# Block quantisation of the FFN weights: all vector passes on VectorE, the rounding constant in one ScalarE pass

## The reference

```python
def _quantize_elem(x, ebits, mfrac, max_norm):
    ax = jnp.abs(x)
    priv = jnp.floor(jnp.log2(jnp.where(ax == 0, 1.0, ax)))
    priv = jnp.maximum(priv, float(-2 ** (ebits - 1) + 2))
    scale = jnp.exp2(priv - mfrac)
    return jnp.clip(jnp.round(x / scale) * scale, -max_norm, max_norm)

def _quantize_mx(x, ebits, mfrac, emax_elem, max_norm):
    xb = x.reshape(shp[:-1] + (shp[-1] // 32, 32))
    amax = jnp.max(jnp.abs(xb), axis=-1, keepdims=True)
    sexp = jnp.floor(jnp.log2(jnp.where(amax == 0, 1.0, amax))) - emax_elem
    scale = jnp.exp2(jnp.clip(sexp, -127, 127))
    return (_quantize_elem(xb / scale, ebits, mfrac, max_norm) * scale).reshape(shp)

def _q_w(w): return _quantize_mx(w, 2, 1.0, 2.0, 6.0)
gate = einsum(_q_act(x), _q_w(w_gate)); up = einsum(_q_act(x), _q_w(w_up))
out = x + einsum(_q_act(silu(gate) * up), _q_w(w_down))      # w_gate, w_up: 2048 x 512, w_down: 512 x 2048
```

## Time and profile before

| | us |
|---|---|
| time, median of 3 runs | 645.82 |
| lowest and highest of the 3 | 642.88, 647.63 |
| span of the profiled execution (first to last instruction) | 645.2 |
| front, to the first weight unit on DVE | 30.0 |
| step 0 | 47.7 |
| steps 1 to 6 | 294.0, or 49.0 each |
| from step 7's start to the first matmul of the FFN | 47.3 |
| FFN | 226.3 |

### The profile page before, as it was taken

The page is one execution under the profiler, slowest core; times in us unless marked ns, Lnnn a source line. Parts: engine busy times, 40 slices in busy tenths (PEclk is TensorE's granted clock), DMA queues, the critical chain, the costliest instruction groups (busy, mean ns, idle before and its releaser), DMA issues.

```text
span 645.2 us, 11064 instructions
## 1 busy us (share of the span) xinstructions
PE 512.5 (79%) x2992; PEld 322.8 (50%) x2992; DVE 567.9 (88%) x951; ACT 387.4 (60%) x803; POOL 388.1 (60%) x391
## 2 busy tenths in 40 slices
PE   1799688777599789689599785569998899889984
PEld 1375565655575665565475653424444444344431
DVE  1347899999999999999999999669999999999994
ACT  2478778787678788688687777323334333343332
POOL 6367577687678678677677677643343434444443
PEclk9958768688778588688777687679999999999997
DMA  5220303203203203212312101010111000210020
GB/s 158 99 99 20 113 19 123 87 15 118 84 15 116 81 30 106 89 33 98 98 33 98 65 1 46 5 49 2 33 48 49 33 33 33 65 33 33 33 65 34
DMA packets 25479, 38.48 MB, mean 60 GB/s; under 512 B 4848, under 2 KB 8944, under 8 KB 25456
## 3 DMA queue, kind: packets, MB, share of 16 engines
...
...
## 4 chain that ended last, share of the span: by engine, by line
issue 31%; DVE 31%; PE 25%; ACT 9%; POOL 2%; DVEq 1%; DMA 1%; POOLq 0%; ACTq 0%; SPq 0%
PE psA L1168 5%; PE psA L1194 5%; PE psA L1359 3%; PE psC L1136 3%; DVE wam L884 3%; DVE f L932 2%; PE psC L1227 2%; DVE qam L884 2%; ACT Dt L684 2%; DVE CT L956 2%; DVE wn L912 2%; DVE qs L887 2%; DVE qinv L890 2%; PE psC L1218 1%; PE psC L1376 1%
## 5 line engine op out<-in xcount | busy, mean ns | idle before, releaser
L587 POOL TENSOR_TENSOR qd<-qc,qs 128x512 bf16<-128x512 bf16 x64 | 67.1, 1048 | 121.4 <-DVE qc L1104 121.4
L828 ACT ACTIVATE wraw<-psA 128x512 f32<-128x512 f32 x64 | 38.1, 598 | 107.4 <-PE psA L1359 105.5
L1194 PE MATMUL psA<-vp,CT 128*128 128x33 f32 x512 | 83.3, 320 | 24.3 <-DVE CT L956 24.1
L1194 PEld LDWEIGHTS psA<-vp,CT 128*128 128x128 f32 x512 | 80.4, 243 | 29.6 <-issue 17.6
L1168 PE MATMUL psA<-qbd,kT 128*128 128x512 f32 x128 | 72.6, 719 | 0.4 <-issue 0.4
L684 ACT ACTIVATE Dt<-psB,gT 128x128 f32<-128x128 f32 x256 | 71.1, 377 | 0.2
L1359 PE MATMUL psA<-WgT,xqT 128*128 128x512 bf16 x256 | 68.3, 391 | 1.7 <-ACT WdT L677 1.1
L482 POOL TENSOR_TENSOR wq<-wn,ws 128x1024 bf16<-128x1024 bf16 x24 | 45.9, 1912 | 38.3 <-DVE wn L913 38.3
L1376 PE MATMUL psC<-WdT,pTs 128*128 128x512 bf16 x256 | 67.6, 388 | 0.0
L1359 PE MATMUL psA<-WuT,xqT 128*128 128x512 bf16 x256 | 67.5, 387 | 0.0
L489 POOL TENSOR_TENSOR wy<-wm,wy 128x1024 f32<-128x1024 f32 x24 | 63.2, 2633 | 1.0 <-ACT wm L666 1.0
(11 more groups left out here) (128 smaller groups left out, 1152.4 us busy)
## 6 DMA issues: line engine op xcount, KB each, us to landing
...
```

What stands on the lines that cost most here:

```text
L587: nc.gpsimd.tensor_tensor(blocks(qd[k][:, :]), blocks(qc[k][:, :]), spread(qs4[k][:, :], QB), ALU.mult).then_inc(pq_ready.sem, 1)
L1194: last = nc.tensor.matmul(psA[:, i4, j * VW:(j + 1) * VW], CT[n % 2][:, j * P:(j + 1) * P], vp[p][:, c, HPC * i4 + j, :], start=True, stop ...
```

## The change

Five things change in the first part of the program.

1. The three POOL passes of a unit (`scale_w`, `add_w`, `back_w`) leave POOL's block and its list.
2. On DVE, `w_front` takes the place of `w_scale` and ends with the full-tile multiply into `wy`. `w_round` becomes two `scalar_tensor_tensor` passes of 128 x 1024: `wy = max(wy, W_LOW) + wm`, then `wn = min(wy, W_HIGH) - wm`, which hold the clamp as well as the addition and the subtraction. `w_back` is new and makes `wq`.
3. `w_pow` has one operation in place of two, in one pass as before.
4. `round_const` on ACT is one Identity pass in place of two.
5. DVE's list is written in another order: `w_round(0)` stands before `c_mult(2)` in place of behind `c_mult(3)`, `w_back(0)` before `c_mult(3)`, and `w_round(2)` and `w_back(2)` before `c_mult(7)` in place of behind `split`.

```diff
-INV_W = float((254 - 20) << 23)
+W_UNIT = 2.0 ** -4
+INV_W = float(252 << 23)
+W_SLOPE = 2.0 ** 22 * 0.8125
+W_BASE = 2.0 ** 23 * 0.5625 * W_UNIT
+W_LOW = -6.0 * W_UNIT
+W_HIGH = (2.0 ** 23 * 2.1875 + 6.0) * W_UNIT
-W_OUT = -(2.0 ** 20)
+W_OUT = 1.0 / (4.0 * W_UNIT)
...
-            def scale_w(b, u):
-                nc.gpsimd.tensor_tensor(blocks(wy[wb][:, :]), blocks(wraw[u][:, :]), spread(winv[wb][:, :], UB),
-                                        ALU.mult).then_inc(y_ready.sem, 1)
-            def back_w(b, u):
-                nc.gpsimd.tensor_tensor(blocks(wq[wb][:, :]), blocks(wn[wb][:, :]), spread(ws4[wb][:, :], UB),
-                                        ALU.mult).then_inc(wq_ready.sem, 1)
-            def add_w(b, u):
-                nc.gpsimd.tensor_tensor(wy[wb][:, :], wm[wb][:, :], wy[wb][:, :], ALU.add).then_inc(r_ready.sem, 1)
...
-                ch.link(nc.scalar.activation(wm[wb][:, :], wm[wb][:, :], ACT.Relu, bias=neg15[:, 0:1], scale=2.0 ** 22))
-                nc.scalar.activation(wm[wb][:, :], wm[wb][:, :], ACT.Identity,
-                                     bias=pos15[:, 0:1]).then_inc(m_ready.sem, 1)
+                nc.scalar.activation(wm[wb][:, :], wm[wb][:, :], ACT.Identity, scale=W_SLOPE,
+                                     bias=wbase[:, 0:1]).then_inc(m_ready.sem, 1)
...
+            def w_front(b, u):
                 ve.wait_ge(w_ld[u], 16 * b + 16)
                 ch.link(reduce_blocks(wraw[u][:, :], wam[wb][:, :]))
                 ch.link(power(wam[wb][:, :], ws4[wb][:, :]))
-                inverse(ws4[wb][:, :], winv[wb][:, :], INV_W).then_inc(inv_ready.sem, 1)
+                ch.link(inverse(ws4[wb][:, :], winv[wb][:, :], INV_W))
+                nc.vector.tensor_tensor(blocks(wy[wb][:, :]), blocks(wraw[u][:, :]), spread(winv[wb][:, :], UB),
+                                        ALU.mult).then_inc(y_ready.sem, 1)
...
             def w_round(b, u):
-                ch.link(nc.vector.tensor_tensor(wn[wb][:, :], wm[wb][:, :], wy[wb][:, :], ALU.subtract))
-                nc.vector.tensor_scalar(wn[wb][:, :], wn[wb][:, :], W_MAX, -W_MAX, ALU.min,
-                                        ALU.max).then_inc(wn_ready.sem, 1)
+                ch.link(nc.vector.scalar_tensor_tensor(out=wy[wb][:, :], in0=wy[wb][:, :], scalar=W_LOW, in1=wm[wb][:, :],
+                                                       op0=ALU.max, op1=ALU.add))
+                nc.vector.scalar_tensor_tensor(out=wn[wb][:, :], in0=wy[wb][:, :], scalar=W_HIGH, in1=wm[wb][:, :],
+                                               op0=ALU.min, op1=ALU.subtract).then_inc(wn_ready.sem, 1)
+            def w_back(b, u):
+                nc.vector.tensor_tensor(blocks(wq[wb][:, :]), blocks(wn[wb][:, :]), spread(ws4[wb][:, :], UB),
+                                        ALU.mult).then_inc(wq_ready.sem, 1)
```

More of the change, by code:

```diff
@@ L136, in bass_mlstm_cross_attention__mx_ffn_kernel @@
         mhalf = sb("mhalf", [P, 2])
-        neg15 = sb("neg15", [P, 1])
-        pos15 = sb("pos15", [P, 1])
+        wbase = sb("wbase", [P, 1])
         WgT = sb("WgT", [P, HC, INNER], BF16)
@@ L548, in step @@
             def step(b, p, first, more):
-                scale_w(b, 0)
                 if not first:
@@ L903, in w_pow @@
                 ve.wait_ge(y_ready.sem, y_ready.at(b, u + 1))
[L904 to L905 removed]
+                nc.vector.tensor_scalar(wm[wb][:, :].bitcast(I32), wy[wb][:, :].bitcast(I32), EXPO, None,
+                                        ALU.bitwise_and).then_inc(pow_ready.sem, 1)
             def w_round(b, u):
                 wb = u % 2
[L909 to L914 removed]
+                ve.wait_ge(m_ready.sem, m_ready.at(b, u + 1))
+                ch.link(nc.vector.scalar_tensor_tensor(out=wy[wb][:, :], in0=wy[wb][:, :], scalar=W_LOW, in1=wm[wb][:, :],
[3 more added lines that the diff above has]
+            def w_back(b, u):
+                wb = u % 2
+                ve.wait_ge(wn_ready.sem, wn_ready.at(b, u + 1))
+                ve.wait_ge(wT_mm.sem, wT_mm.at(b, u - 1 if u >= 2 else 0))
+                nc.vector.tensor_tensor(blocks(wq[wb][:, :]), blocks(wn[wb][:, :]), spread(ws4[wb][:, :], UB),
+                                        ALU.mult).then_inc(wq_ready.sem, 1)
             def x_stats(b):
@@ L1022, in step @@
             def step(b, p, first, more):
-                w_scale(b, 0)
+                w_front(b, 0)
                 if more:
                     x_stats(b + 1)
+                w_pow(b, 0)
                 if not first:
                     head_var(b - 1, 1 - p, 1)
-                w_pow(b, 0)
                 if more:
                     x_aggregate(b + 1)
-                w_scale(b, 1)
+                w_front(b, 1)
                 c_mult(b, 0)
+                w_pow(b, 1)
                 c_mult(b, 1)
@@ L1035, in step @@
                     head_norm(b - 1, 1)
+                w_round(b, 0)
                 c_mult(b, 2)
-                w_pow(b, 1)
+                w_back(b, 0)
                 c_mult(b, 3)
-                w_round(b, 0)
                 if not first:
@@ L1042, in step @@
                 head_var(b, p, 0)
-                w_scale(b, 2)
+                w_front(b, 2)
                 c_mult(b, 4)
+                w_pow(b, 2)
                 head_norm(b, 0)
-                w_pow(b, 2)
+                w_round(b, 1)
                 if not first:
                     x1_round(b - 1, 1)
+                w_back(b, 1)
                 c_mult(b, 5)
-                w_round(b, 1)
+                w_round(b, 2)
                 c_mult(b, 6)
+                w_back(b, 2)
                 c_mult(b, 7)
@@ L1056, in step @@
                     split(b + 1)
-                w_round(b, 2)
                 combine(b, p)
```

31 lines of the change are left out of this document (2 added, 29 removed).

## The result

The changed kernel takes 656.04 us (median of 4 runs, 655.61 to 658.22), beside 645.66 us for the kernel before on the same chip (642.88 to 647.63). The ratio is 1.015, with a 95% interval of 1.012 to 1.019: slower, by 10.4 us. The profiled execution of the changed kernel took 655.61 us, with a span of 653.7; that of before had a span of 645.2, which is 8.5 us less.

A forecast was written before the change was run, and what follows sets the result against it. DVE's list was taken to bound the kernel, at 49.0 us a step growing to 51.0. The span of 645.2 + 12.0 (steps 1 to 6) - 1.7 (step 0) + 2.9 (step 7) gave 658.4, with 0.6 to the median 659 us; range 640 to 668.

The forecast's parts named there:

- What bounds the kernel: In steps 1 to 6 DVE is busy 95%, so a step lasts as long as DVE's list, 49.0 us.
- Blocks by the moved passes: On DVE, time held by the nine POOL passes that the change removes goes: -10.2 us a step.
- Work put in: New DVE passes cost 4.66 us a unit, less 1.59 taken out: net 9.2 us a step.
- New blocks: POOL's remaining passes hold DVE's new list, mainly the second pass of `w_round`: 4.4 us a step.
- A new wait: DVE idles at `head_var(b, 0)` for the heads' copy and square, with only `x1_stats` as cover: 2.0 us a step.
- Small terms: Two small blocks inside `x1_round` and the 0.3 us wait for Dt go: about -0.6 us a step.
- Step 0: Waits for POOL's multiply and for Dt go or shrink, against the added work: -1.7 us.
- Step 7: `c_mult(7)` comes later, and part is given back behind it: +2.9 us.
- `c_mult(7)` comes 5.0 us later: In step 7, because all three units are then finished ahead of it: 5.0 us.
- Gives back 2.1: In step 7 behind `c_mult(7)`, the wait for POOL and `w_round(2)` are gone: 2.1 us back.
- rival 1: Freed port outweighs the added passes, remaining blocks 2.8 us and `head_var` wait covered: step 48.0 us, 637 us; chance 0.20.

The follow-up runs named there:

- e3: The kernel before with only the addition taken off POOL, scaling and multiplication back staying there; 632.57 us.
- e7: e3 with `w_round(b, 1)` moved ahead of `x1_round(b - 1, 1)` in DVE's list; 631.92 us.
- e9: The kernel before with addition and scaling taken off POOL, the multiplication back staying there, in the order of before; 643.66 us.
- e5: The changed kernel with `w_back(0)` behind `c_mult(3)` and `w_front(2)` ahead of `head_var(b, 0)`; 643.01 us.
- e1: The changed kernel with `w_round(0)` and `w_back(0)` moved back behind `c_mult(3)`; 651.59 us.
- e11: All three passes off POOL as in the change, in the order of the kernel before, but with the scaling placed as in e10; 637.25 us.
- e12: The changed kernel in its own order, with only the scaling moved: behind `x_stats`, `c_mult(0)` and `c_mult(4)` for units 0, 1 and 2; 656.31 us.
- e10: e9 with only the scaling moved: behind `head_var(b - 1, 1)`, `c_mult(1)` and `c_mult(4)` for units 0, 1 and 2; 627.4 us.
- e8: e3 with the multiplication back also taken off POOL, on DVE behind each `w_round`, the scaling staying on POOL; 637.87 us.

## Why the prediction was right, by its own steps

The forecast was 659 us and the kernel takes 656, slower as said, and in the main for the reasons said. That it came within 3 us is in part luck: the sum put 12.0 us on steps 1 to 6 where 7.9 were measured, and the difference of the medians is 1.9 us over that of the profiled spans. Term by term:

- **What bounds the kernel** (DVE's list). It fits both kernels: DVE is busy 95% and 91% of steps 1 to 6, and half of its idle time in the changed kernel is the wait at `head_var`. It is no longer so at 42 us of busy time a step, in the order of e3 (e7).
- **Blocks by the moved passes, -10.2 us.** L873 and L967 came down to 0.68 us, L954 to 0.18 and `decay`'s L907 to 0.38. e3 shows that the addition was the cause for L904 and L932, and e9 that the scaling was for `head_norm`: 2.12 us on average in e3, 0.68 in e9.
- **Work put in, +9.2 us.** 1.22 for a `scalar_tensor_tensor` of this size was right (1.209 shortest).
- **New blocks, +4.4 us.** Held time is the mean less the shortest, times the count: 2.6 us a step at L881, 0.5 at L879, 0.5 at L888, mostly at the passes named, and 0.6 at a small pass that the prediction didn't name (L987, held by POOL's `weigh`, or L856, held by `back_x`): 4.2 us on average over steps 1 to 6. The 0.4 each at `w_pow(1)` and `decay` did not occur. So the sum was right in part by luck, as the pass that was not named stands for two that did not come.
- **A new wait, +2.0 us.** 2.25 us, in every step, on "ACT hf" with the reduction behind it. e5, which takes it away, gains 1.7 us a step; e1 shows that a wait of 2.25 us isn't worth 2.25 us if its cover is taken from another wait.
- **Small terms, -0.6 us.** Mis-sized, and this is the term that made the forecast step too long. They were 0.3 for `Dt`, and in `x1_round` the blocks at L890 (0.55 us on average against 0.175 in the changed kernel, twice a step) and L887 (0.33 against 0.175): 0.75 and 0.3, where 0.3 stood for both. So they are -1.35, and the working gives 45.2 + 4.2 + 2.25 - 1.35 = 50.3, which was measured, against 51.0 forecast.
- **Step 0, -1.7 us.** -1.6.
- **Step 7, +2.9 us.** +4.7. The larger error is in "`c_mult(7)` comes 5.0 us later": counted from the start of the step it ended at 33.6 us before (405.26) and ends at 40.0 now (415.71), 6.4 later. "Gives back 2.1" was too large as well: from there to the FFN are 13.6 us before and 12.0 now, 1.65 less, since with nothing between `c_mult(7)` and `combine` but `x1_stats`, `combine` waits 3.36 us for the last heads.
- **Not in the sum: the front, -2.3 us.** DVE's list there did not change, but the first eight `wgt` matmuls took 3.62 us before and 1.90 after:

```profile
17.78 3.62 PE L1227 MATMUL psC<-qT,wgt 128*48 128x256 f32 x8 [0.78 <-ACT kT L658]
```
```profile
17.39 1.90 PE L1205 MATMUL psC<-qT,wgt 128*48 128x256 f32 x8 [0.80 <-ACT kT L629]
```

The other 0.5 us are in the matmuls just ahead of and behind these. It is not an effect of the change: of the 14 kernels profiled, ten have 3.6 us here and start step 0 at 29.7 to 30.3 us, e11 with all the instructions of the change among them, and four (the changed kernel, e5, e7 and e12) have 1.90 us and start it at 27.7 to 27.9. In step 4 of e9 and e10 eight such matmuls took 3.57 us at a granted clock of 0.50 and 1.93 at 1.00; here, however, the profile gives a granted clock of 1.00 for both kernels, so it does not say why they differ. The errors of the front and of step 7 nearly cancel in the sum.

Two slips of the prediction change nothing in it. The 10.2 us are what all nine POOL passes of a step held, not one pass. And the point from which rival 1 holds, blocks and wait together under 3.8 us, leaves out the small terms; with them it is 4.4 as forecast, and 5.2 as measured, where blocks and wait came to 6.45.

**The rivals.** Rival 1, 637 us, was worked out as "the remaining blocks stay at 2.8 us and the wait is covered". e11 comes near that: 637.25 us, 47.5 us a step where the rival had 48.0, and 0.8 us of waits at `head_var` in six steps. What kept the change from it is its order, not its arithmetic. Neither rival nor forecast had a lever in it that is as large as the cost of the change: where the scaling stands against `c_mult`, 14 us in e11 and 16 in e10. In e12 it gave nothing. That fits the step being set there by the wait at `head_var` and by DVE's own list, but the place is not quite the same: in e12 the scaling of unit 0 stands ahead of `head_var(b - 1, 1)` and that of unit 1 ahead of `c_mult(1)`, in e11 behind both, and no run tells the two reasons apart.

The Trainium skill (Perfetto Trace Analysis, section Optimizing Scalar/DVE Operations) says that moving work between the engines that share the port might not help. Here it depends on the pass: beside one another in one order (e3, e9, e8), DVE took the addition for 4.2 us of busy time *less* a step, the scaling for 0.2 less, the multiplication back for 2.4 more.
